# A start-up rewritten by hand: V weights in quarters, zero-tile matmuls, x and V tiles between halves of Q, K and G

## What is computed

```python
xn  = layernorm(x)
q   = elu(xn @ W_Q.T) + 1          # 8 heads of 64
k   = elu(xn @ W_K.T) + 1
v   = xn @ W_V.T
# linear attention with decay, step t:
S   = g * S + k_t v_t^T;   z = g * z + k_t
y_t = (S q_t) / (z . q_t + 1e-6)
gate = sigmoid(xn @ W_g.T + b_g)
attn = (y * gate) @ W_O.T
# mixture: router picks 2 of 8 experts of rank 4
ffn  = xn @ W_lin.T + b_lin + sum_top2(weight * (xn @ left) @ right)
out  = x + attn + ffn
```

## Time and profile before

| what | value |
|---|---|
| median of 3 runs | 256.4 us (256.15 to 257.37) |
| the profiled execution, its own time | 256.4 us |
| its span on the slowest core (first to last instruction) | 255.4 us |
| spans of the eight cores | 253.7 to 255.4 us |
| PE busy | 237.1 us (93% of the span) |
| PE weight loads, DVE, ACT, POOL busy | 118.3, 164.3, 75.6, 59.9 us |
| DMA | 36.90 MB, mean 145 GB/s |

### The profile page before, as it was taken

One profiled execution on the slowest core, in us unless ns is written; L12 is line 12 of the kernel. 1 busy time (PEld: TensorE's weight loads), 2 busy tenths in 40 slices (PEclk: granted clock), 3 DMA queues, 4 the chain that ended last, 5 costly groups with the idle time before them and its releaser, 6 DMA issues.

```text
span 255.4 us, 5316 instructions; the slowest of 8 cores (253.7 to 255.4 us)
## 1 busy us (share of the span) xinstructions
PE 237.1 (93%) x1701; PEld 118.3 (46%) x1701; DVE 164.3 (64%) x430; ACT 75.6 (30%) x128; POOL 59.9 (23%) x95
## 2 busy tenths in 40 slices
PE   0179999999979999999999999999999999999996
PEld 0144444455544555454444455454545555545443
DVE  3776674948947678667565657546566776787522
ACT  2646857486254322414232021111111111000000
POOL 0069200021325411414050403021214030444000
PEclk9999999999999999999999999999999999999999
DMA  6999999999999055343424122323222323135433
GB/s 150 286 278 246 239 172 172 264 179 187 205 212 320 3 146 166 63 166 62 167 43 165 42 83 85 104 82 105 83 103 85 104 85 123 62 131 201 167 124 122
DMA packets 20222, 36.90 MB, mean 145 GB/s; under 512 B 12194, under 2 KB 12770, under 8 KB 19684
## 3 DMA queue, kind: packets, MB, share of 16 engines
q1 hardware_dynamic: 17876, 26.99, 34.0%
q0 software_dynamic: 2320, 9.59, 19.4%
HBM read 32.00 MB, written 8.39 MB: 158 GB/s over the span
## 4 chain that ended last, share of the span: by engine, by line
PE 86%; DMA 4%; DVE 4%; issue 2%; ACT 1%; SPq 1%; DVEq 0%; ACTq 0%
PE PJ L376 27%; PE L L398 18%; PE L L442 9%; PE PJ L369 9%; DMA wlin_sb<-wv 4%; PE L L376 3%; PE PJ L398 3%; PE SY L390 2%; PE T L347 2%; PE SY L414 2%; PE T L428 1%; PE SY L418 1%; PE T L436 1%; PE PJ L442 1%; PE T L355 1%
## 5 line engine op out<-in xcount | busy, mean ns | idle before, releaser
L398 PE MATMUL L<-wlin_sb,xnfm 128*128 128x512 bf16 x208 | 49.2, 379 | 0.0
L334 POOL TENSOR_SCALAR S_blk<-S_sb,small_s 128x260 bf16<-128x260 f32 x30 | 28.8, 973 | 81.5 <-DVE S_sb L879 81.5
L398 PEld LDWEIGHTS L<-wlin_sb,xnfm 128*128 128x128 bf16 x208 | 20.0, 98 | 24.3 <-issue 1.0
L696 DVE TENSOR_SCALAR e_sb<-e_sb 128x512 bf16<-128x512 bf16 x32 | 9.9, 308 | 29.6 <-ACT e_sb L957 29.6
L957 ACT ACTIVATE e_sb<-PJ 128x512 bf16<-128x512 f32 x28 | 16.5, 592 | 40.6 <-PE PJ L376 39.4
L376 PE MATMUL PJ<-xnfm,wk_sb 128*128 128x512 bf16 x112 | 26.6, 380 | 1.4 <-ACT th_g L964 1.4
L933 ACT ACTIVATE xn_tm<-x_sb,nmr,rstd 128x1024 bf16<-128x1024 f32 x16 | 19.9, 1241 | 26.0 <-POOL nmr L292 24.5
L442 PE MATMUL L<-wo_sb,ygfm 128*128 128x512 bf16 x104 | 26.7, 379 | 0.0
L376 PE MATMUL PJ<-xnfm,wg_sb 128*128 128x512 bf16 x112 | 26.6, 379 | 0.0
L376 PE MATMUL PJ<-xnfm,wq_sb 128*128 128x512 bf16 x112 | 26.6, 380 | 0.0
L369 PE MATMUL PJ<-wv_sb,xnfm 128*128 128x512 bf16 x96 | 24.6, 400 | 1.7 <-DVE wv_sb L691 1.7
(11 more groups left out here) (136 smaller groups left out, 339.3 us busy)
## 6 DMA issues: line engine op xcount, KB each, us to landing
ro_sb<-x SPq DMA_DIRECT2D x16, 512.0 KB, 3.4
out<-ro_sb SPq DMA_DIRECT2D x15, 512.0 KB, 2.7
x_sb<-x SPq DMA_DIRECT2D x10, 512.0 KB, 9.1
x_sb<-x POOLq DMA_DIRECT2D x6, 512.0 KB, 14.6
wlin_sb<-wv SPq DMA_DIRECT2D x2, 1024.0 KB, 13.1
wlin_sb<-wlin POOLq DMA_DIRECT2D x1, 2048.0 KB, 40.1
wq_sb<-wq POOLq DMA_DIRECT2D x2, 512.0 KB, 11.0
wk_sb<-wk POOLq DMA_DIRECT2D x2, 512.0 KB, 20.1
```

Source lines behind the costliest of these rows:

```text
L334: GP.tensor_scalar(S_blk[:, :].rearrange("p (q w) -> p q w", q=4)[:, :, 65 * e : 65 * e + 65], S_sb[:, :].rearrange("p (q w) -> p q w", q= ...
L398: TE.matmul(lb(c, n)[:, :], xnk(k, c), wlin_sb[:, D * k + 512 * n : D * k + 512 * n + 512], start=False, stop=False)
L696: VE.tensor_scalar(e_sb[:, 512 * i : 512 * i + 512], e_sb[:, 512 * i : 512 * i + 512], 1.0, None, ALU.min).then_inc(dv_m, 1)
```

## The change

SP's queue: x3 goes ahead of the V weights; these are loaded in four quarters of 0.5 MB, with the two constants after the second. POOL's queue: its first DMA waits for x3 in place of the first V weights, and x4 to x7 are put between the halves of the weights. PE: ten matmuls of 128x512 on the zeroed tile `S_blk` (`warm`) run around the transpose of chunk 1; V of chunks 0 to 2 follows the quarters; each of x4 to x7 is transposed between quarters of Q, K or G; V4 to V7 stand between Q, K, the two halves of G, and behind G, each in a bank of its own (`vb`); the router product stands ahead of the last quarter of G. DVE and ACT follow that order. In the loop's thin slots ACT runs `tanhg` ahead of `xn`.

```diff
+    vb = ring4 + [SYb[0], SYb[1], SYb[0], T1f]
...
+        def load_wv(i):
+            o = 2 * FH * i
+            SY.dma_start(wv32[:, o : o + 2 * FH],
+                         wv_d[:, o : o + 2 * FH]).then_inc(d_wv[i], 16)
...
         load_x(2)
+        load_x(3)
         load_wv(0)
-        load_x(3)
         load_wv(1)
         SY.dma_start(small[:, :], small_d[:, :]).then_inc(d_sm, 16)
         SY.dma_start(cmat, cmat_d[:, :]).then_inc(d_cm, 16)
+        load_wv(2)
+        load_wv(3)
...
-        GP.wait_ge(d_wv[0], 16)
+        GP.wait_ge(d_x[3], 16)
         wload_half(wq_sb, wq_d, 0, d_wq)
         xload(4)
+        wload_half(wq_sb, wq_d, 1, d_wq)
+        wload_half(wk_sb, wk_d, 0, d_wk)
         xload(5)
-        wload_half(wq_sb, wq_d, 1, d_wq)
+        wload_half(wk_sb, wk_d, 1, d_wk)
         xload(6)
         xload(7)
-        wload_half(wk_sb, wk_d, 0, d_wk)
-        wload_half(wk_sb, wk_d, 1, d_wk)
+        wload_half(wg_sb, wg_d, 0, d_wg)
         wload(lg_sb, lg_d, d_lg)
-        wload_half(wg_sb, wg_d, 0, d_wg)
         wload_half(wg_sb, wg_d, 1, d_wg)
...
+    def warm(n):
+        for _ in range(n):
+            TE.matmul(SYb[0][:, :], S_blk[:, 0:128], S_blk[:, 0:512], start=True, stop=True)
...
         xtr(0)
+        TE.wait_ge(dv_ini, 3)
+        warm(4)
         xtr(1)
+        warm(6)
         TE.wait_ge(dv_xev, 1)
+        xtr(2)
         for i in range(2):
             TE.wait_ge(dv_cast, i + 1)
-            vproj(0, ring4[0], 2 * i, 2 * i + 2)
-        xtr(2)
-        TE.wait_ge(dv_xev, 2)
-        vproj(1, ring4[1], 0, 4)
+            for c in range(2):
+                TE.wait_ge(dv_xev, c + 1)
+                vproj(c, vb[c], 2 * i, 2 * i + 2)
         TE.wait_ge(dv_xev, 3)
-        vproj(2, ring4[2], 0, 4)
+        vproj(2, vb[2], 0, 4)
+        xtr(3)
         for i in range(2, 4):
             TE.wait_ge(dv_cast, i + 1)
-            vproj(0, ring4[0], 2 * i, 2 * i + 2)
-        xtr(3)
-        vproj(1, ring4[1], 4, 8)
-        vproj(2, ring4[2], 4, 8)
+            for c in range(3):
+                vproj(c, vb[c], 2 * i, 2 * i + 2)
         TE.wait_ge(dv_xev, 4)
-        vproj(3, ring4[3])
+        vproj(3, vb[3])
...
             if more and lo < 0:
                 SE.wait_ge(pe_k, c + 5)
                 eexp(9 + 2 * c, PJ[1])
                 vev(c + 8, PJ[0])
+                tanhg(b + 1, s, PJ[1])
             if c + 10 < NCH:
                 xn(c + 10)
...
-            if more:
+            if more and lo >= 0:
                 tanhg(b + 1, s, PJ[1])
```

More of the change, by code:

```diff
@@ L141, in build_core @@
     d_lg = sem("d_lg")
-    d_wv, d_wq, d_wk, d_wg = ([sem("d_wva"), sem("d_wvb")], [sem("d_wqa"), sem("d_wqb")],
+    d_wv, d_wq, d_wk, d_wg = ([sem(f"d_wv{i}") for i in range(4)], [sem("d_wqa"), sem("d_wqb")],
                               [sem("d_wka"), sem("d_wkb")], [sem("d_wga"), sem("d_wgb")])
@@ L530, in pe_program @@
             fproj(wq_sb, 0, m, ring4[m], pe_q, 0, 4)
-        TE.wait_ge(dv_xev, 3)
-        xtr(4)
         TE.wait_ge(d_wq[1], 16)
         for m in range(4):
+            if m == 2:
+                xtr(4)
             fproj(wq_sb, 0, m, ring4[m], pe_q, 4, 8)
[L536 to L541, removed]
+        TE.wait_ge(dv_xev, 5)
+        vproj(4, vb[4])
         TE.wait_ge(d_wk[0], 16)
         for m in range(4):
[L544 to L548, removed]
+            TE.wait_ge(dv_q, m + 1)
+            fproj(wk_sb, 0, m, ring4[m], pe_k, 0, 4)
         TE.wait_ge(d_wk[1], 16)
         for m in range(4):
-            fproj(wk_sb, 0, m, ring4[(m + 2) % 4], pe_k, 4, 8)
-        xtr(6)
+            if m == 2:
+                xtr(5)
+            fproj(wk_sb, 0, m, ring4[m], pe_k, 4, 8)
         TE.wait_ge(dv_xev, 6)
-        xtr(7)
+        vproj(5, vb[5])
         TE.wait_ge(d_wg[0], 16)
         for m in range(4):
+            if m == 3:
+                xtr(6)
             TE.wait_ge(dv_k, m + 1)
-            fproj(wg_sb, 0, m, ring4[(m + 2) % 4], pe_g, 0, 4)
+            fproj(wg_sb, 0, m, ring4[m], pe_g, 0, 4)
+        TE.wait_ge(dv_xev, 7)
+        TE.wait_ge(ac_v, 5)
+        vproj(6, vb[6])
         TE.wait_ge(d_wg[1], 16)
         for m in range(4):
[L561 to L568, removed]
+            if m == 1:
+                xtr(7)
+            if m == 3:
+                TE.wait_ge(dv_xev, 8)
+                TE.wait_ge(d_lg, 16)
+                tgp(0)
+            fproj(wg_sb, 0, m, ring4[m], pe_g, 4, 8)
+        vproj(7, vb[7])
         for c in range(NCH):
@@ L574, in pe_program @@
             if c == 0:
+                TE.wait_ge(ac_g, 3)
                 TE.wait_ge(ac_v, 7)
@@ L625, in pe_program @@
                 if c == 0:
-                    TE.wait_ge(dv_xev, 8)
+                    TE.wait_ge(ac_v, 8)
                 elif c != 3:
@@ L689, in cast_wv @@
         o = 2 * FH * i
-        VE.wait_ge(d_wv[i // 2], 16)
+        VE.wait_ge(d_wv[i], 16)
         VE.tensor_copy(wv_sb[:, o : o + 2 * FH], wv32[:, o : o + 2 * FH]).then_inc(dv_cast, 1)
@@ L808, in dve_program @@
         stats(4)
+        phi(0, ring4[0], fm(qfm, 0)[:, 0:512], dv_q)
+        xev_v(4)
+        for m in range(1, 4):
+            phi(m, ring4[m], fm(qfm, 0)[:, 512 * m : 512 * m + 512], dv_q)
         stats(5)
[L810 to L817, removed]
         VE.wait_ge(ac_dec, 3)
         qt(0)
-        for m in range(4):
-            phi(4 + m, ring4[(m + 2) % 4], fm(kfm, 0)[:, 512 * m : 512 * m + 512], dv_k)
+        stats(6)
+        phi(4, ring4[0], fm(kfm, 0)[:, 0:512], dv_k)
+        xev_v(5)
+        for m in range(1, 4):
+            phi(4 + m, ring4[m], fm(kfm, 0)[:, 512 * m : 512 * m + 512], dv_k)
+        stats(7)
         xev_v(6)
@@ L988, in act_program @@
         SE.activation(nlg[:, :], nlg[:, :], AF.Ln, bias=one_c[:, :]).then_inc(ac_dec, 1)
-        for c in range(3):
-            vev(c, ring4[c])
+        for c in range(4):
+            vev(c, vb[c])
         SE.wait_ge(dv_dec, 2)
@@ L1004, in act_program @@
             eexp(m, ring4[m])
[L1005 to L1008, removed]
+        SE.wait_ge(dv_mk, 1)
+        SE.activation(masks[:, :], mtmp, AF.Exp).then_inc(ac_mk, 1)
+        vev(4, vb[4])
+        xn(5)
         for m in range(4):
             SE.wait_ge(pe_k, m + 1)
-            eexp(4 + m, ring4[(m + 2) % 4])
-        SE.wait_ge(dv_mk, 1)
-        SE.activation(masks[:, :], mtmp, AF.Exp).then_inc(ac_mk, 1)
+            eexp(4 + m, ring4[m])
+        xn(6)
+        vev(5, vb[5])
+        xn(7)
+        vev(6, vb[6])
         for m in range(4):
-            tanhg(0, m, ring4[(m + 2) % 4])
+            tanhg(0, m, ring4[m])
         xn(8)
         e8exp(0)
-        vev(6, L[0])
-        vev(7, L[1])
+        vev(7, vb[7])
         xn(9)
```

14 lines of the change are left out of this document (4 added, 10 removed).

## The result

The changed kernel takes 260.59 us (median of six runs; 258.55 to 261.00 for five of them), the kernel before took 256.88 us beside it: a ratio of 1.012 with a 95% interval of [1.007, 1.017], which is +3.0 us on 256.4. The sixth run took 302.05 us, with the four cores of one die at a granted clock of 0.82 to 0.88; such runs are left out of every ratio and count here. The forecast was 259.3 us, slower. The profiled execution took 258.85 us, with 257.8 us of span on core 4, the slowest.

What follows compares the result with a forecast made beforehand. PE was taken to bound the kernel: its start, rate and waits. +3.9 (last quarter), +0.4 (V to router) and -1.4 (tanh) gave +2.9 on 256.4, so 259.3 us, range 254.4 to 263.8.

Steps and rivals of the forecast that it cites:

- Delay of the last quarter: V phase: POOL's packets alternate with those of V quarters 2 and 3; quarter 3 lands at 26.2, V ends +3.9 us.
- not held to one for one: SP's queue at the start: the constants' small packets are not paired with POOL's packets; 5.0 us of pairing taken, bound 12.4.
- The clock: Rival, V phase: PE idles before quarters 2 and 3 and returns at 1.2 GHz, 3.0 to 4.2 us more; chance 0.22.
- V to the router: From V's end to the router's end: V6 and G's order add 0.87, Q's middle stall goes; net +0.4 us.
- Router to av: From the router's end to the first av: DVE's chain keeps its 8.6 us, PE's wait about 1.4; cost 0.
- The tanh: Loop slot 1: tanh ahead of xn runs in ACT's idle time, so K no longer waits for it; -1.4 us.
- The zero matmuls: Around the transpose of chunk 1: 4.3 us in PE's gaps, saving nothing of their own as the last quarter sets the end.
- The undisturbed rival: V phase: quarters not disturbed, quarter 3 at 21.2, Q stalls 0.7 for wq1; sum -1.5, 254.9 us; chance 0.18.
- The rival of turns of many rows: DMA engines take the quarters' 16 rows in one turn; V ends 0.7 later, sum -0.3, 256.1 us; chance 0.15.

Runs made afterwards that it cites:

- the old kernel's collision: The kernel before, with only POOL's first DMA made to wait for x2 in place of the first V half: 260.10 us, 1.0140.
- the halves: The changed kernel with V's weights as two halves of 1 MB, the constants between them, in place of quarters: 258.37 us, 1.0092.
- the run that kept the clock: The changed kernel with more zero matmuls in the two gaps before quarters 2 and 3: 258.46 us, 1.0088.
- after: The changed kernel itself, as against before, the kernel without the change: 260.59 us, ratio 1.012.
- the changed kernel again: The changed kernel, unedited, timed again beside the kernel before: 259.25 us, 1.0104.

## Why the prediction was right

The total came out right (+3.0 us by the ratio, +2.45 in the profiled execution, +2.9 forecast), but by luck: two of its terms were wrong and of opposite sign. The delay of the last quarter was put about 3 us too high, and the fall of the clock, left out of the sum, cost 2.8 us on the slowest core.

**Delay of the last quarter, +3.9: the mechanism right, the size not.** "16 of POOL's go between them ... That is 5.0 us, and quarter 3 lands at 26.2." The mechanism, V's quarters held up by POOL's packets, is shown by two runs: take most of the overlap away and 0.9957 is left, make it in the old kernel and it alone gives 1.014. The size was put too high: the last cast starts at 23.12 on the slowest core and at 23.3 in the mean, not at 26.2.

What failed is when POOL's packets come, not how they share an engine. The forecast had POOL's first issue at 13.4 and its rate at 17.1, 3.7 us behind; the issue came at 11.48 on core 4 (11.5 to 13.3 over the cores), and the count that was read as the rate in the earlier trace rows, some 60 packets in 2 us, came in 18 to 20, 7.5 us behind it. Here POOL's first packet moves 3.75 to 4.75 us after the issue, in the kernel before 1.75 to 3.75. In the mean of the cores the issue moved forward by 1.9 us, the first packet by 0.4. So quarter 2 came with little or no delay on five cores (its cast at 17.61 on core 4, where 22.5 was forecast), and only the rows that SP still had were held up. After 16 us these are 155 packets on core 4, just under ten an engine, against the 16 that the forecast paired. Ten of POOL's are wq0's eight and two of x4's, 4.0 us by the forecast's prices; quarter 3 is 5.5 us behind quarter 2, where 2.0 is the undisturbed distance, so 3.5 us late. The three cores on which quarter 2 was late too (0, 3 and 5) are nearest to the forecast's picture, with last casts at 24.24, 23.70 and 25.01; on cores 0 and 3 the counts in 18 to 21 us are 103 of SP's to 87 of POOL's, and 94 to 98.

The reading that small packets are "not held to one for one" was wrong as well: in the run with the old kernel's collision the constants are, 51 to 51. It cost nothing here: the constants stand ahead of quarter 2, and when POOL's first packets came only 155 of SP's were left, fewer than the 256 rows of the two quarters.

**The clock, forecast as a rival at 0.22: it did fall, on half of the core executions.** On core 4 it costs 2.8 us and brings V's end to 29.80, against 29.95 forecast. "No row of before shows a fall after 2 to 3 us" is true of that trace, but no ground for leaving the term out: in other runs the clock fell after idle times of that length (2.05 us on core 5 of the halves). Here the gap was 3.72 us, since quarter 2 came early and the two gaps became one. The rival's price, 14 matmuls with 0.21 us more each, was right on core 4 (2.8 us); on core 1 it was 1.7. What it had wrong was the delay under it.

**V to the router, +0.4.** Measured +0.2: 28.0 us from Q's start to the end of the router (29.80 to 57.80) against 27.8.

**Router to av, 0.** 66.43 - 57.80 = 8.6 us, as forecast, with a wait of 1.3 us at its end (1.4 forecast).

**The tanh, -1.4.** From the first av to the end of the span 191.4 us remain (257.8 - 66.43), against 192.8 before: -1.4, and the run with this move alone gives the same. ACT's timeline, for the earlier trace rows:

```profile
70.97 0.69 ACT L973 ACTIVATE th_g<-PJ,gb_h 128x512 f32<-128x512 f32 x1 [1.15 <-PE PJ L379]
72.94 1.24 ACT L942 ACTIVATE xn_tm<-x_sb,nmr,rstd 128x1024 bf16<-128x1024 f32 x1 [1.29 <-POOL nmr L295]
```

It runs in idle time ahead of xn, which waits for POOL behind it as before.

**The zero matmuls, nothing.** As forecast; the run without them shows no difference in time.

**The undisturbed rival, 254.9.** It is what the kernel becomes with the wait one transfer later: 255.25, Q waiting for wq for 0.4 to 1.5 us on six cores, 0.7 forecast. The rival's picture was right, its condition (POOL's data later than SP's last rows) was not met in the changed kernel. What it had right is that POOL's data come later than its issue suggests.

**The rival of turns of many rows.** It gave 256.1. The one-for-one counts of the old kernel's collision speak against it, and the last casts at 21.3 to 25.0 too.

**Why the slowest core loses more than the mean.** Q starts 2.6 us later in the mean of eight cores, and with +0.2 and -1.4 about 1.4 us of span would follow; the mean over cores and runs rose by 1.9 (254.4 to 256.3). The kernel's time is the slowest core's, and its span rose by about 3.5 us (255.3 to 258.9, mean over runs): last casts that scatter over 3.7 us instead of 1.4, and clocks that fall on some cores, widen the distance of the slowest from the mean. The prediction reckoned with one core and did not see this.

**Open.** Why POOL's first packets come later after their issue when SP's queue is full, and what makes the clock fall after one idle time and not after another of the same length, is not shown; nor is how the loss divides between late data and clock: the fallen cores are 2.2 us longer, but the run that kept the clock regained at most part of that in its ratio.

## What to carry to other kernels

When a second queue is started early, ask which last rows of the first are still in flight, and what hangs on them, and read from the packet counts whether its own data come any earlier: one semaphore decided here between 0.996 and 1.010 of the old time, and both a step too early and one too late lost. A transfer that gates TensorE costs more than its delay if the granted clock falls in the idle time before it, so look at the clock row first where a start has moved. And time such an edit alone: here 1.4 us of gain from a two-line move lay hidden in a change that lost 3 us in all.

## What the runs showed of the hardware

- **A queue issued behind a busy one starts late.** POOL's first packet moved 3.75 to 5.0 us after its first issue on all 16 cores of the two traces in which it was issued at 9.9 to 13.3 us, with SP's V rows still ahead (after, and the old kernel's collision). In the kernel before it was 1.75 to 3.75 us, and 1.25 to 3.0 in the run with POOL waiting for the second quarter, issued at 16.0 to 17.4.
- **Two full queues move as many packets each, whatever their size.** In the old kernel's collision core 1 moved 31 to 31, 43 to 43 and 51 to 51 packets in three microseconds, of 0.13 to 0.05, 0.15 to 0.02 and 0.18 to 0.02 MB.
- **Few remaining rows can be late.** In 20 to 24 us of core 4 SP's queue moved 16 packets beside 247 of POOL's, and the last V quarter's cast waited for them until 23.12.
- **The clock falls on single cores.** The lower level (0.50 to 0.52 over stretches of 2 us) followed PE's idle times of 3.72 and 3.19 us (cores 4 and 1 of after), 3.13 (core 0 of the run with more zero matmuls), 2.90 (core 0 of the run without any), 2.88 (core 7 of the changed kernel again), 2.85 and 2.05 (cores 1 and 5 of the halves) and 2.07 (core 3 of the old kernel's collision). It did not follow 2.91 (core 6 of after), 2.90 (core 5 of the changed kernel again), 2.52 (core 5 of the old kernel's collision), or 2.08 and 1.95 close together (core 5 of after).
- **A slow start does not show in the granted clock.** The pitch of 0.43 us at the start of the program stands beside a granted clock of 1.00 in both kernels (15 to 20 us before, 9 to 12 us after), where the later fall shows as 0.53.
